# Choosing experts by comparison, finding a slot's tile by rounding, and scales one tile earlier in a layer of attention and a mixture of experts

## The reference, cut to what matters

```python
# x: 4 x 256 x 256; c: 4 x 256; wmod: 256 x 1536
mod = (silu(c) @ wmod).reshape(4, 6, 1, 256)      # sa, ca, ga, sb, cb, gb, one row for each batch
h = layernorm(x) * (1 + ca) + sa
x = x + ga * attention(h)                         # linear attention: A = sum_s K/|K| * V; (A * Q) W_out + h
h = layernorm(x) * (1 + cb) + sb                  # 1024 tokens of 256
logits = h @ router_w.T                           # 8 experts
probs = softmax(logits); w, idx = top_k(probs, 2); w = w / sum(w)
for e in range(8):                                # F = 704
    out += silu(h @ Wg[e].T) * (h @ Wu[e].T) @ Wd[e].T * comb[:, e:e+1]
x = x + gb * out
```

## Time and profile before

| | us |
|---|---|
| median of 3 runs | 288.37 |
| lowest, highest | 287.08, 288.47 |
| the profiled execution, its own time | 287.14 |
| its span, first to last instruction | 285.3 |
| PE busy, DVE busy | 234.7, 172.4 |
| ACT busy, POOL busy | 151.0, 135.6 |

### The profile page before, as it was taken

How to read it: one execution, slowest core, us unless ns; L and a number is a source line. 1 busy time by engine, 2 the same in 40 slices (tenths; PEclk the granted TensorE clock), 3 DMA queues, 4 the chain that set the end, 5 groups by cost and what they waited for, 6 DMA issues and landing times.

```text
span 285.3 us, 5001 instructions
## 1 busy us (share of the span) xinstructions
PE 234.7 (82%) x1404; PEld 156.9 (55%) x1405; DVE 172.4 (60%) x419; ACT 151.0 (53%) x275; POOL 135.6 (48%) x180
## 2 busy tenths in 40 slices
PE   1898999497964226699989999998899999999970
PEld 1525667256754213367656656665567766666650
DVE  2248689469789999395765755755744444434420
ACT  2114694587566904486766767765543343334410
POOL 1028669249945018204564564564544454545222
PEclk9999997889575555789999999999999999999995
DMA  7994276607630208847457454322333232233211
GB/s 260 343 412 196 67 239 207 249 2 220 241 110 1 74 0 274 290 148 224 104 163 215 82 153 137 68 32 53 83 52 62 57 59 55 55 55 65 31 19 18
DMA packets 15729, 36.91 MB, mean 129 GB/s; under 512 B 1941, under 2 KB 9493, under 8 KB 15706
## 3 DMA queue, kind: packets, MB, share of 16 engines
q1 hardware_dynamic: 9978, 26.09, 26.5%
q0 software_dynamic: 5152, 9.08, 16.9%
q10 hardware_dynamic: 576, 1.46, 1.4%
HBM read 31.49 MB, written 6.19 MB: 132 GB/s over the span
## 4 chain that ended last, share of the span: by engine, by line
PE 35%; issue 21%; DMA 14%; DVE 14%; POOL 9%; POOLq 2%; ACT 2%; SPq 1%; DVEq 0%
PE bank L689 13%; PE bank L715 8%; DMA out<-shared,dest_i 6%; DMA staged<-in_w 5%; POOL rows L1345 4%; DMA W<-in_wmod 3%; PE bank L526 3%; PE bank L699 2%; PE bank L492 2%; DVE W L958 2%; POOL x L1345 2%; PE bank L572 2%; POOL unscale L1353 1%; POOLq L1351 1%; PE bank L537 1%
## 5 line engine op out<-in xcount | busy, mean ns | idle before, releaser
L689 PE MATMUL bank<-W,x 128*128 x414 | 89.2, 371 | 1.3 <-ACT x L882 0.9
L1379 POOL DMA_INDIRECT out<-shared,dest_i x23 | 36.5, 1587 | 80.2 <-DVE shared L1236 80.2
L689 PEld LDWEIGHTS bank<-W,x 128*128 128x128 f16 x414 | 41.2, 100 | 43.5 <-issue 6.2
L1226 DVE SCALAR_TENSOR_TENSOR shared<-bank,unscale,x 128x256 f32<-128x256 f32 (+1 forms) x69 | 28.1, 456 | 48.0 <-ACT x L888 48.0
L888 ACT ACTIVATE x<-bank,unscale 128x256 f32<-128x256 f32 (+1 forms) x69 | 27.1, 455 | 49.6 <-POOL unscale L1353 38.5
L715 PE MATMUL bank<-W,shared 128*128 x414 | 51.0, 276 | 2.2 <-DVE shared L1249 1.7
L715 PEld LDWEIGHTS bank<-W,shared 128*128 128x128 f16 x414 | 39.7, 99 | 8.7 <-issue 2.9
L763 ACT ACTIVATE W<-staged,w_scale_bits 128x1408 f16<-128x1408 f32 (+1 forms) x24 | 35.9, 1500 | 13.0 <-DVE w_scale_bits L947 11.2
L958 DVE SCALAR_TENSOR_TENSOR W<-staged,w_scale_bits,W 128x1408 f16<-128x1408 f32 (+1 forms) x24 | 41.7, 1746 | 0.2
L756 ACT ACTIVATE W<-staged 128x1408 bf16<-128x1408 f32 (+1 forms) x24 | 33.9, 1413 | 11.8 <-DMA staged<-in_w 11.8
L1249 DVE TENSOR_TENSOR shared<-bank,shared 128x512 f16<-128x512 f32 (+1 forms) x46 | 23.5, 552 | 15.0 <-ACT shared L897 15.0
(11 more groups left out here) (179 smaller groups left out, 310.4 us busy)
## 6 DMA issues: line engine op xcount, KB each, us to landing
staged<-in_w SPq DMA_DIRECT2D x16, 704.0 KB, 5.7
staged<-in_w SPq DMA_DIRECT2D x8, 768.0 KB, 4.3
token_rows<-mod_rows SPq DMA_DIRECT2D x4, 259.0 KB, 10.4
x<-in_x SPq DMA_DIRECT2D x4, 256.0 KB, 9.3
W<-in_wmod SPq DMA_DIRECT2D x2, 512.0 KB, 8.9
W<-mod_rows SPq DMA_DIRECT2D x4, 256.0 KB, 4.5
out<-x SPq DMA_DIRECT2D x4, 256.0 KB, 4.2
token_rows<-rows SPq DMA_DIRECT2D x4, 256.0 KB, 3.1
```

Source lines behind the costliest of these rows:

```text
L689: mm = pe.matmul(bank[2 + n][:, 0:2 * w], half[:, kc * P:(kc + 1) * P], W1_pairs[:, bass.ds(e * 2 + part, 1), :, kc, n * PIECE:n * PIECE + w],
L1226: ve.scalar_tensor_tensor(act[:, n * PIECE:n * PIECE + w], bank[2 + n][:, w:2 * w], unscale[c % 2][:, 1:2], sig[:, n * PIECE:n * PIECE + w ...
L1379: po.indirect_dma_start(out, bass.IndirectOffsetOnAxis(dest_i[:, j:j + 1], 0), y_sb[r], None, bounds_check=last_row, oob_is_err=True, comp ...
```

## The change

1. **Experts by comparison.** Each logit is compared with the seven others of its token: `above` counts how many exceed it (a tie goes to the lower index by a smallest number in a constant table). Chosen is what has fewer than 2 above. This is done for the first six tiles as soon as three batches' logits are there, and for the last two when the fourth batch is. The running sums of the first six are made in between; the last two cost two short additions. Rank and count matmuls use 16-bit copies of their constants (`tri16`, `part16`).
2. **Tile of a slot by rounding.** Adding and subtracting 1.5 * 2^23 rounds the slot (shifted by a constant) to its tile: 16 elements. The table product needs 24 columns, and its result is the token number plus one, with no difference of neighbours. `source_i` and `dest_i` stand ahead of `tile_e`, the expert order and the greatest logit with its exponent.
3. **Work moved behind the routing.** `low(1, 2)` and `power_scale(2, W2_OF)` go behind the expert order; `norm(2, W2_OF)` behind the count. The softmax weights' matmuls and their read-out go into tile 0's turn. ACT takes `row_high(3)` ahead of `high(3, 0)`, waits for the logits' difference only after `squares(3, 2)`, and has only `high(2, 2)` between the exponent and `slots_out(0)`; `high(3, 2)` follows that. `squares(4, 0)` and `squares(4, 1)` go into tile 0's turn behind its `sig`, and all the `TILE_*` steps about a third to one tile later.
4. **Scales a tile further ahead.** `unscale` has a ring of four. POOL makes `unscales(j+3)` and `slot_weights(j+3)` in tile j's turn.
5. **POOL's rows wait.** `rows(1)` and `rows(2)` wait for the normalised tile of the batch after (`xn2_ok`).
6. **Modulation.** PE does `keys_values(0, *)` ahead of `mod_rows`; DVE does `mods_a` ahead of `first_norm(1)`. `ga_b` and `mod_b` are filled by one DMA each, and the gates of all 1024 rows by one DMA, issued from ACT's queue.

```diff
@@ SP
-            for b in range(B):
-                sp.dma_start(of_batch(ga_b, b), modrow_d[b:b + 1, 0:D].to_broadcast([P, D])).then_inc(s["ga_in"], 16)
-            for b in range(B):
-                sp.dma_start(of_batch(mod_b, b), modrow_d[b:b + 1, D:3 * D].to_broadcast([P, 2 * D])).then_inc(s["modb_in"], 16)
-            for b in range(B):
-                sp.dma_start(rows_d[b * S:(b + 1) * S, GATE:], modrow_d[b:b + 1, 3 * D:].to_broadcast([S, D + 3])).then_inc(s["gates_out"], 16)
+            sp.dma_start(v3(ga_b, B), modrow_d[:, 0:D].rearrange("(a b) d -> a b d", a=1).to_broadcast([P, B, D])).then_inc(s["ga_in"], 16)
+            sp.dma_start(v3(mod_b, B), modrow_d[:, D:3 * D].rearrange("(a b) d -> a b d", a=1).to_broadcast([P, B, 2 * D])).then_inc(s["modb_in"], 16)
@@ ACT
+            def gates_of_batches():
+
+                sc.wait_ge(s["modrow_out"], 16)
+                sc.dma_start(rows_d[:, GATE:].rearrange("(b p) n -> b p n", b=B),
+                             modrow_d[:, 3 * D:].rearrange("b (a n) -> b a n", a=1).to_broadcast([B, S, D + 3])).then_inc(s["gates_out"], 16)
...
             weighted_out(0)
+            gates_of_batches()
             modulated(2)
...
             row_high(2)
+            row_high(3)
             high(3, 0)
-            row_high(3)
+            high(3, 1)
+            squares(3, 2)
             sc.wait_ge(s["sub_ok"], 1)
             sc.activation(expo, logit_less_max, ACT.Exp).then_inc(s["expo_ok"], 1)
             sc.activation(warm[:], keep[:, 0:1], ACT.Silu)
-            high(3, 1)
             high(2, 2)
-            squares(3, 2)
-            high(3, 2)
...
             slots_out(0, 0)
-            squares(4, 0)
-            squares(4, 1)
+            high(3, 2)
             turns(sc, tile_step)
@@ DVE
+            def chosen(start, n, read):
+
+                cols = slice(start * E, (start + n) * E)
+                ins = ve.tensor_copy(logits[:, cols], logits_p[:, cols])
+                if read:
+                    ins.then_inc(s["early_ok"], 1)
+                    ve.wait_ge(s["early_ok"], 1)
+                else:
+                    link(ins)
...
+                link(ve.tensor_tensor(over.rearrange("p (t e f) -> p t e f", e=E, f=E), of, against, ALU.subtract))
+                link(ve.tensor_tensor(v3(over, n), v3(over, n), bc_mid(keep[:, C_OVER:C_OVER + E * E], n), ALU.is_gt))
+                link(ve.tensor_reduce(above[:, cols], v3(over, n * E), AX.X, ALU.add))
+                ve.tensor_scalar(tiles_sum[0][:, SUM0 + start * E:SUM0 + (start + n) * E], above[:, cols], 2.0, None,
+                                 ALU.is_lt).then_inc(s["sel_ok"], 1)
+
+            ve.wait_ge(s["r_done"], B - 1)
+            chosen(0, EARLY, True)
...
+            power_scale(3, W1_OF)
+            row_low(2)
+
+            ve.wait_ge(s["r_done"], B)
+            chosen(EARLY, TB, False)
...
+            link(ve.tensor_scalar(slot_tile[:], slot[:], ROUND, ROUND, ALU.add, ALU.subtract))
...
+            ve.wait_ge(s["table_done"], 1)
+            ve.tensor_scalar(source_i[:], table_p, -1.0, 0.0, ALU.add, ALU.max).then_inc(s["source_ok"], 1)
@@ POOL
+                if 1 <= b < B - 1:
+                    po.wait_ge(s["xn2_ok"], b + 2)
...
-                if j + 2 < SLOT_TILES:
-                    tile_scales(j + 2)
+                if j + 3 < SLOT_TILES:
+                    slot_weights(j + 3, unscales(j + 3))
```

More of the change, by code:

```diff
@@ L240, in layer @@
         slot_hi, slot_lo = slot16[:, 0:D], slot16[:, D:2 * D]
-        unscale = [sb(f"unscale{r}", 2) for r in range(2)]
+        unscale = [sb(f"unscale{r}", 2) for r in range(4)]
         slot_weight = [sb(f"slot_weight{r}", 2) for r in range(4)]
@@ L247, in layer @@
         chosen_part = under(W2, 6 * W2_EXP + 4 * P)
-        logit_less_max, expo, left, slot_all = [chosen_part(NR) for _ in range(4)]
+        logits, logit_less_max, expo, slot_all, above = [chosen_part(NR) for _ in range(5)]
+        margin = chosen_part(EARLY * E * E)
         choice, picked = [chosen_part(2 * NR) for _ in range(2)]
@@ L252, in layer @@
         ahead, ahead_steps, at_place = [chosen_part(E * E) for _ in range(3)]
-        top = [sb(f"top{n}", TT) for n in range(2)]
-        top_rev = sb("top_rev", TT)
+        top = sb("top", TT)
         weight = sb("weight", PAIRS)
@@ L603, in _ @@
             turn_x(0)
+            pe.wait_ge(s["win_in"], 16)
+            keys_values(0, 0)
+            keys_values(0, 1)
             pe.wait_ge(wmod_in[1], 16)
@@ L749, in _ @@
             sc.activation(ident16[:], keep[:, C_ID:C_ID + P], ACT.Copy).then_inc(s["ident_ok"], 1)
+            sc.activation(tri16[:], keep[:, C_TRI:C_TRI + P], ACT.Copy).then_inc(s["halves_ok"], 1)
+            sc.activation(part16[:], keep[:, C_PART:C_PART + P], ACT.Copy).then_inc(s["halves_ok"], 1)
             def squares(e, m):
@@ L1120, in _ @@
             second_normed(3)
-            power_scale(3, W1_OF)
-            low(1, 2)
-            power_scale(2, W2_OF)
             ve.tensor_scalar(pad_row[:], keep[:, C_TOKEN:C_TOKEN + 1], float(TOKENS), None, ALU.add)
@@ L1152, in _ @@
+            power_scale(3, W1_OF)
+            row_low(2)
+            ve.wait_ge(s["r_done"], B)
+            chosen(EARLY, TB, False)
+            ve.wait_ge(s["sel_ok"], 2)
+            for t in range(EARLY, TT):
+                at = SUM0 + t * E
+                ins = ve.tensor_tensor(tiles_sum[3][:, at:at + E], tiles_sum[3][:, at - E:at], tiles_sum[0][:, at:at + E], ALU.add)
+                if t < TT - 1:
                     link(ins)
@@ L1154, in _ @@
                     ins.then_inc(s["sums_ok"], 1)
-            row_low(2)
+            for n in range(2):
+                ve.tensor_scalar(choice[:, n * NR:(n + 1) * NR], above, float(n), None, ALU.is_equal)
             row_low(3)
@@ L1191, in _ @@
             ve.tensor_copy(order_i[:], order[:]).then_inc(s["order_ok"], 1)
-            ve.wait_ge(s["table_done"], 1)
-            link(ve.tensor_copy(table[:, 0:NT + 1], table_p))
-            link(ve.tensor_tensor(filled[:], table[:, 0:NT], table[:, 1:NT + 1], ALU.subtract))
-            ve.tensor_scalar(source_i[:], filled[:], -1.0, 0.0, ALU.add, ALU.max).then_inc(s["source_ok"], 1)
-            link(ve.tensor_scalar(nobody[:], filled[:], 0.5, pad_row[:, 0:1], ALU.is_lt, ALU.mult))
-            link(ve.tensor_tensor(nobody[:], nobody[:], filled[:], ALU.add))
-            ve.tensor_scalar(dest_i[:], nobody[:], -1.0, None, ALU.add).then_inc(s["dest_ok"], 1)
+            link(ve.tensor_reduce(top[:], v3(logits, TT), AX.X, ALU.max))
+            ve.tensor_tensor(v3(logit_less_max, TT), v3(logits, TT), bc_last(top[:], E), ALU.subtract).then_inc(s["sub_ok"], 1)
+            power_scale(2, W2_OF)
+            low(1, 2)
+            power_scale(3, W2_OF)
+            low(3, 0)
             ve.wait_ge(s["expo_ok"], 1)
@@ L1244, in tile_step @@
                     low(*unit)
-                if c >= 1:
+                if c == 0:
+                    slot_weights()
+                else:
                     result(i, c - 1, (c - 1) % 2)
```

174 lines of the change are left out of this document (81 added, 93 removed).

## The result

| | before | after |
|---|---|---|
| median, lowest to highest, us | 288.42, 287.08 to 290.85 | 265.21, 264.90 to 265.75 |
| the profiled execution, its span | 287.14, 285.3 | 264.90, 263.1 |
| busy PE, DVE | 234.7, 172.4 | 223.3, 172.3 |
| busy ACT, POOL | 151.0, 135.6 | 155.2, 138.3 |

The change makes the kernel 8.1% faster: the ratio is 0.919, with a 95% interval of 0.914 to 0.925. The prediction was 268.5 us (range 264.5 to 276.0), so 18.6 us of gain were forecast and 22.2 came. The sign was right, and all four gains came; three of their sizes were off, in both directions, so that the total came nearer than its terms.

What follows compares the result with a forecast made beforehand. Taken as bounds: PE's 6.5 us a tile, plus 0.76 lost in tiles 2 to 12 to late `unscale`, and the chain to tile 0. 4.1 + 5.5 + 2.6 + 6.4 = 18.6; 287.14 - 18.6 = 268.5 us, range 264.5 to 276.

Steps and rivals of the forecast that it cites:

- all four gains: Gates 4.1 us, routing 5.5, tiles 0 and 1 2.6, tiles 2 to 12 6.4; all coming had chance 0.5.
- the upper bounds of two terms: Whole kernel: the basis given for the range's lower end, 264.5 us.
- gates, to the end of `keys_values(3, *)`: Front: unit 5 lands sooner once the gates leave SP's queue, so PE's keys start earlier; 4.1 us, bounds 0 to 5.4.
- normalising (1.9), comparison (1.7), tile of a slot (2.0): Routing: `source_i` comes 5.5 us earlier, 3.6 from normalising and comparison, 2.0 from rounding; bounds 4.0 to 6.5.
- `source_i` to `gate_up(0)`: Ahead of tile 0: steps moved behind `source_i` delay the exponent; 6.7 us for 6.4, a loss of 0.3.
- I give 0.2 for that: PE's `keys_values(3, *)`: running faster than 5.16 us without idle time ahead of them gains 0.2 us.
- Unit 5 comes no earlier: Rival in the front: one copy over fewer DMA engines leaves unit 5 landing at 52.8; 272.6 us, chance 0.2.
- the queues are now two: Argument against the rival "Unit 5 comes no earlier": gates and unit 5 stand in separate queues; no size given.
- DVE is late by 0.9: Routing: DVE ends the early six tiles' work at about 89.2, 0.9 us after the last logit at 88.3.
- if POOL's rows slow DVE's comparison: Lower bound of the routing term: comparison slowed as normalising was, gain 4.0 us for 5.5.
- The step "6.4": Tiles 2 to 12: scales a tile further ahead bring 79.88 to 73.7 us; gain taken 6.4, bounds 3.0 to 7.5.
- Tiles keep their pace: Rival in tiles 2 to 12: scatter, gather, result bind, so tiles stay at 7.26 us; 275 us, chance 0.1.

Runs made afterwards that it cites:

- rows_first: The kernel after with PE's `mod_rows` ahead of `keys_values(0, *)` again, the old order; 265.13 us, ratio 0.924 to before.
- gates_sp1: The kernel after with the gates' single DMA on SP's queue ahead of unit 5, not on ACT's; 276.55 us, ratio 0.963 to before.
- at_once: The kernel after with the comparison of all eight tiles in one piece after the last logit; 265.49 us, ratio 0.929 to before.
- gates_late: The kernel after with the gates' single DMA on ACT issued later, behind `weighted_out(3)`; 266.19 us, ratio 0.923 to before.
- scales_two: The kernel after with `unscale` and slot weights made two tiles ahead, not three; 276.69 us, ratio 0.963 to before.
- the two pool runs: The kernel after with POOL's rows waiting for DVE's normalising at batch 2 only (266.68 us, ratio 0.922) or never (266.60 us, ratio 0.925).
- before_gates: The kernel before with only the gates' edit, one DMA on ACT's queue; 280.06 us, ratio 0.978 to before.
- routing_alone: The kernel after with gates back in four pieces on SP's queue and `unscale` two tiles ahead; 280.55 us, ratio 0.979 to before.
- before_scales_three: The kernel before with only `unscale` in a ring of four, made three tiles ahead; 277.20 us, ratio 0.966 to before.
- the six other profiles: Profiles of rows_first, gates_late, the two pool runs, at_once, and after with gates as four DMAs on SP; tiles 2 to 12 take 73.3 to 73.8 us.

## Why the prediction was nearly right, point by point

The 22.2 us by which the spans differ, cut at the same events. The total is better than its terms: the gates' column brought 4.4 too much, the routing and tiles 2 to 12 together 3.4 too little, and that they met is luck. The range was luck in part too: its lower end, 264.5, was said to be the upper bounds of two terms, but the two largest of these add 1.4 and 1.3 and end at 265.8, above the 265.21 measured; 264.5 takes three.

| term | predicted | in the two profiles |
|---|---|---|
| gates, to the end of `keys_values(3, *)` | 4.1 (0 to 5.4) | 8.5 |
| to the last normalising | 0 | 0.1 |
| normalising (1.9), comparison (1.7), tile of a slot (2.0) | 5.5 (4.0 to 6.5) | 3.4 |
| `source_i` to `gate_up(0)` | -0.3 | 0.0 |
| tiles 0 and 1 | 2.9 | 3.6 |
| tiles 2 to 12 | 6.4 (3.0 to 7.5) | 5.1 |
| tiles 13 on | 0 | 1.5 |

**Gates.** The mechanism was right and the term too small. The wait of 3.88 before the keys went and they take 3.60: 5.4, the upper bound. My "I give 0.2 for that" was the mis-sized step; it is 1.56. The slow 5.16 us go with a lower clock behind idle time: in before the granted clock is 0.50 from 56 to 58 us, after PE had stood idle, and in after it is 1.00 from 48 to 52. Where PE comes to these keys from other work they take 3.60 or 3.70 in every profile, and 5.16 to 6.46 where it stood idle for 3.9 us or more before them.

The other 3 us of the 8.5 are `queries(0)` (1.4 earlier) and `queries(2)` (2.84 for 4.40), and the second is the clock again: 0.73 and 0.50 over 44 to 48 us in before, 1.00 in after. It fell between 42 and 50 us in every profile but those of after, rows_first and gates_sp1. So the keys start at 48.71 in after and 49.13 in rows_first, but at 50.82 to 51.76 in at_once, gates_late, scales_two and the two pool runs (part of that is `queries(0)`, which start up to 1.4 us later there), and the first column is 54.4 to 55.4 there, for 52.3. Some 2 to 3 us of the 8.5 belong to the profiled execution, then, and not to the gates; compared at equal clocks they are worth the 4.9 to 6.0 of before_gates and of routing_alone with scales_two. Why the clock stayed up in these profiles is open. The rival "Unit 5 comes no earlier" named four engines as the condition; the four engines came (by the share of 0.27), and that form is what let unit 5 through. Against it I had written "the queues are now two", which alone would not have sufficed.

**Routing.** The shortfall of 2.1 is in the comparison, and in normalising the last batch (the last logit comes 1.3 us earlier behind its start, not 1.9). From the last logit to the count step DVE takes 5.4 us (80.43 to 85.86), and 5.3 before (90.25 to 95.59). "DVE is late by 0.9" was 2.9. The early part took 7.7 us from the end of normalising, and I had counted 5.0: a wait of 0.70 for the third batch's logits (76.55) was not in it; the three 384-number steps, counted at 0.6 each from an instruction of 400 that ran when POOL was idle, took 2.7 for 1.8; the rest is small steps at 0.5 beside POOL. Yet the bound below, "if POOL's rows slow DVE's comparison", named the case, and it was the likelier one, since the earlier trace rows show POOL's rows starting right there. Once DVE is late, the last batch's fast normalising gains nothing more either; the forecast added 1.9 and 1.7 as if each were on the path. By the Trainium skill, SBUF — State Buffer, section Who interferes with whom, a DVE step with two SBUF inputs contends with a GpSimd instruction that reads SBUF, and a reduction never contends. The rows after agree: 1.50 for the one, 0.55 for the other. But a step with one input was slowed as well: L1155 takes 0.55 beside POOL's rows, and 0.17 on the last two tiles. The tile by rounding gave 2.2 of its 2.0: the count step to the end of `source_i` takes 7.05 for 9.22.

**To `gate_up(0)`.** As predicted, with 6.4 for 6.7: the exponent's table load ran inside ACT's wait, the second took 1.28, and neither showed a drain.

**Tiles 0 and 1.** 3.6 for 2.9. `turn_act(0)` follows the end of `gate_up(0)` (105.25) after 0.97, 3.09 before.

**Tiles 2 to 12.** The step "6.4" mixed two things: the look-ahead, worth 8.0 to 8.5, and the work that the change moves into these tiles, 4.9 us of DVE and 5.1 of ACT, which I costed at nothing. What else is in the change costs them 1.4 to 2.9; that it is the moved work is argued, and no run moves it alone. The 6.4 itself is not refuted: with the 73.3 to 73.8 of the six other profiles the tiles gain 6.0 to 6.6, and the 5.1 of the table is the low end. In after the loss sits in three tiles, 3, 9 and 11, which take 7.5 or 7.6 us and not 6.6. In each of them `down` starts after a gap that no wait explains, and runs longer (2.13 elsewhere), as here in tile 3's. The three gaps are 1.59 us together, more than half of the 2.9:

```profile
124.74 2.39 PE L719 MATMUL bank<-W,shared 128*128 x18 [0.60 <-issue]
```

In at_once, rows_first and gates_late such gaps stand in tiles 3 and 11, in before_scales_three in none. What they are stays open. The rival "Tiles keep their pace" is refuted by before_scales_three.

**Up to the normalising.** The wait at batch 1 gives 1.46 that I had not counted, and in after only 0.1 of it is seen: the second column is 22.6 in after and rows_first, and 21.6 or 21.7 in routing_alone, scales_two, gates_late and at_once. In after and rows_first PE reaches the end of the keys some 2 us sooner, ACT then waits 1.8 us for unit 6 (0.26 in at_once, not at all in scales_two) and PE 0.6 us for ACT. So part of the front's lead is lost again to unit 6; that was not tried by itself.

**Tiles 13 on.** I predicted 0 and got 1.5. It is the look-ahead too: the last column is 74.7 to 74.9 where the scales are three ahead, 75.4 to 76.3 where they are two.

## What to carry to other kernels

A DMA that nobody waits for can still hold one back that an engine needs: look at what moves in the stretch of the wait, and try queue and form together, since here the queue alone kept a third of the gain and the form alone none of it. When two engines are slowed by each other, cost new steps at the slowed duration if the other engine's work stands beside them, and don't add two gains on one engine's chain: once it is late, only the larger counts. And when a change carries several parts, the difference of one stretch is their sum: tiles 2 to 12 gained 5.1 by a part worth 8 and a loss of near 3 elsewhere. Compare several profiles of the same code before giving a stretch's difference to an edit: here 2 us of the front belonged to one execution, most of them to its clock.
